# Order of the work in the first token group: rank sums ahead of the last adapter pieces, third x tile and table products earlier

## What is computed

```python
# layer 0: a channel mixing chosen per batch (64x64 weights applied to the token axis), then a dense layer
W = weights[condition]; h = einsum('bct,bcd->bdt', x, W)
base = einsum('bsd,od->bso', h, W_base) + b_base
decoded = (h @ enc0) @ (coefs0 * mask0) + (h @ enc1) @ (coefs1 * mask1)   # for each of 3 experts
transformed = real_fourier_orthogonal_multiply(decoded)                    # an inverse real Fourier transform
x = x + base + transformed.sum(axis=0) * 0.5
# layer 1: gated feed-forward, F = 2752, each product with a rank-16 adapter chosen per batch
act = silu(lora(x W_gate, A_gate, B_gate)) * lora(x W_up, A_up, B_up)
down = lora(act W_down, A_down, B_down)
x = x + down @ sign(weight).T + bias
```

## Time and profile before

| | us |
|---|---|
| median of 3 runs | 1940.22 (1938.87 to 1942.41) |
| the profiled execution's own time | 1939.48 |
| its span in the trace | 1937.8 |
| PE busy | 1912.8 (99%) |
| DVE busy | 1493.9 (77%) |
| ACT busy | 767.1 (40%) |
| POOL busy | 542.1 (28%) |

### The profile page before, as it was taken

How to read it: one execution, slowest core, us unless ns; L and a number is a source line. 1 busy time by engine, 2 the same in 40 slices (tenths; PEclk the granted TensorE clock), 3 DMA queues, 4 the chain that set the end, 5 groups by cost and what they waited for, 6 DMA issues and landing times.

```text
span 1937.8 us, 31530 instructions
## 1 busy us (share of the span) xinstructions
PE 1912.8 (99%) x9104; PEld 1608.2 (83%) x9104; DVE 1493.9 (77%) x2493; ACT 767.1 (40%) x1457; POOL 542.1 (28%) x935
## 2 busy tenths in 40 slices
PE   7899999999999999999999999999999999999998
PEld 6788888888988888888898888888889888888887
DVE  7877777778778777777777877777877787777786
ACT  4453333334344343333344434333335443334331
POOL 4542212213415212211523322212061322222100
PEclk9999999999999999999999999999999999999999
DMA  9755445543476554444447555554235655555411
GB/s 241 168 115 109 102 99 115 121 94 82 128 148 126 106 116 99 101 100 87 119 117 143 126 112 111 105 116 99 71 101 131 139 121 111 121 110 113 99 44 44
DMA packets 320629, 218.38 MB, mean 113 GB/s; under 512 B 177192, under 2 KB 311208, under 8 KB 320544
## 3 DMA queue, kind: packets, MB, share of 16 engines
q1 hardware_dynamic: 281952, 188.43, 43.2%
q0 software_dynamic: 36352, 24.19, 6.9%
q10 hardware_dynamic: 2240, 4.72, 0.7%
HBM read 204.35 MB, written 12.58 MB: 112 GB/s over the span
## 4 chain that ended last, share of the span: by engine, by line
PE 90%; DVE 4%; ACT 2%; issue 2%; SPq 1%; DMA 0%; DVEq 0%; ACTq 0%
PE ps L1517 26%; PE ps L1519 25%; PE ps L1518 25%; PE ps L1730 6%; PE ps L1657 2%; PE ps L1577 2%; PE ps L1578 2%; DVE ps L947 2%; PE ps L1543 1%; DVE split L933 1%; PE ps L1541 1%; PE ps L1596 1%; DMA base<-L_ffn_W_base 0%; ACT split L634 0%; ACT hidden L634 0%
## 5 line engine op out<-in xcount | busy, mean ns | idle before, releaser
L1517 PE MATMUL ps<-x,split 128*128 128x512 f32 x1376 | 538.8, 392 | 5.7 <-DVE act_f L1123 4.4
L1519 PE MATMUL ps<-x,split 128*128 128x512 f32 x1376 | 537.0, 390 | 0.0
L1518 PE MATMUL ps<-x,split 128*128 128x512 f32 x1376 | 536.2, 390 | 0.0
L634 ACT ACTIVATE split<-ps 128x512 fp32r<-128x512 f32 x344 | 203.1, 599 | 450.5 <-DVE ps L947 438.4
L526 POOL DMA_DIRECT2D nat_ad<-L_cond_A_down x224 | 136.9, 618 | 736.8 <-DVE ps L947 727.6
L1519 PEld LDWEIGHTS ps<-x,split 128*128 128x128 f32 x1376 | 258.8, 188 | 56.1
L1517 PEld LDWEIGHTS ps<-x,split 128*128 128x128 f32 x1376 | 259.5, 189 | 55.0 <-issue 4.8
L1518 PEld LDWEIGHTS ps<-x,split 128*128 128x128 f32 x1376 | 259.0, 188 | 54.9
L1517 PE MATMUL ps<-hidden 128*128 128x512 f32 x672 | 261.5, 389 | 0.0
L1518 PE MATMUL ps<-hidden 128*128 128x512 f32 x672 | 261.5, 389 | 0.0
L1519 PE MATMUL ps<-hidden 128*128 128x512 f32 x672 | 261.4, 389 | 0.0
(11 more groups left out here) (145 smaller groups left out, 2832.1 us busy)
## 6 DMA issues: line engine op xcount, KB each, us to landing
nat<-L_cond_W_gate SPq DMA_DIRECT2D x336, 128.0 KB
nat<-L_cond_W_up SPq DMA_DIRECT2D x336, 128.0 KB
nat_down<-L_cond_W_down SPq DMA_DIRECT2D x112, 384.0 KB, 6.4
nat_a<-L_ffn_weight SPq DMA_DIRECT2D x128, 128.0 KB, 2.8
nat<-effective_weight SPq DMA_DIRECT2D x24, 512.0 KB
nat<-x SPq DMA_DIRECT2D x16, 512.0 KB
nat_b<-L_cond_B_gate POOLq DMA_DIRECT2D x224, 24.0 KB, 2.2
nat_b<-L_cond_B_up POOLq DMA_DIRECT2D x224, 24.0 KB, 2.1
```

The costliest lines, as they stand in the source:

```text
L634: act.activation(dst, src, func).then_inc(piece_hi, 1)
L1517: pe.matmul(dst, a[0], b[0], start=first, stop=False)
L1518: pe.matmul(dst, a[0], b[1], start=False, stop=False)
L1519: return pe.matmul(dst, a[1], b[0], start=False, stop=last)
```

## The change

Four things are moved, all in the first group; no instruction is added or dropped.

1. SP issues the four loads of the Fourier table and the load of x tile 3 ahead of the six loads of the encoder.
2. ACT and DVE split x tile 2 ahead of the first mixing weights; the coefficient sums and their words come ahead of the first mixing unit's copies; the encoder's words come after x tile 3; `turn_base(1)` comes after the fourth pair of mixing weights, and mixing unit 2's copies after the low-rank words.
3. PE runs the table products ahead of mixing unit 2 instead of unit 3.
4. ACT and DVE do the rank sums after the pieces B 0 and B 1, ahead of B 2 and BREM.

```diff
@@ SP
             for i in range(2):
                 sp.dma_start(coef[i], ...)
                 sp.dma_start(coef_mask[i], ...)
-            for n in range(3):
-                sp.dma_start(enc[R0 * n:R0 * n + R0, :], enc0).then_inc(enc_in, 16)
-                sp.dma_start(enc[3 * R0 + R1 * n:3 * R0 + R1 * n + R1, :], enc1).then_inc(enc_in, 16)
             table_rows = fourier.rearrange("(p c) n -> p c n", c=KC)
             for i in range(4):
                 sp.dma_start(table[:, 2 * i:2 * i + 2], table_rows[:, 2 * i:2 * i + 2]).then_inc(table_in[i], 16)
             load_x(0, 3)
+            for n in range(3):
+                sp.dma_start(enc[R0 * n:R0 * n + R0, :], enc0).then_inc(enc_in, 16)
+                sp.dma_start(enc[3 * R0 + R1 * n:3 * R0 + R1 * n + R1, :], enc1).then_inc(enc_in, 16)
@@ ACT mixing_first
-                for p in range(2):
+                for p in range(3):
                     plain_unit(0, p, NAT_X + p, SPLIT_X + p)
                 for p in range(2):
                     cond(0, p)
-                plain_unit(0, 2, NAT_X + 2, SPLIT_X + 2)
+                low_rank_weights()
+                for e in range(2):
+                    mixing(0, e)
+                cond(0, 2)
+                plain_unit(0, 3, NAT_X + 3, SPLIT_X + 3)
                 act.wait_ge(enc_in, 96)
                 copy(enc_s.rearrange("r k (q d) -> r q k d", q=4),
                      enc.rearrange("r (q k d) -> r q k d", q=4, k=KC)).then_inc(enc_step, 1)
-                mixing(0, 0)
-                low_rank_weights()
-                mixing(0, 1)
-                cond(0, 2)
-                plain_unit(0, 3, NAT_X + 3, SPLIT_X + 3)
-                mixing(0, 2)
                 act.wait_ge(enc_step, 2)
                 act.wait_ge(g_psum, 1)
                 copy(enc[:, 0:512], ps[0:STACK, 6, :]).then_inc(g_moved, 1)
-                mixing(0, 3)
+                for e in range(2, 4):
+                    mixing(0, e)
                 cond(0, 3)
@@ ACT first_layer_all (making) and group
-                    lora_b_tiles(g, 0, "B", 0)
+                    lora_b_tiles(g, 0, "B", 0, range(2))
+                    ranks(g)
+                    lora_b_tiles(g, 0, "B", 0, range(2, PT))
...
-                ranks(g)
+                if g > 0:
+                    ranks(g)
@@ DVE mixing_first
-                for p in range(2):
+                for p in range(3):
                     plain_unit(0, p, NAT_X + p, SPLIT_X + p)
-                for p in range(2):
-                    cond(0, p)
-                plain_unit(0, 2, NAT_X + 2, SPLIT_X + 2)
+                cond(0, 0)
+                adapter_kept()
+                cond(0, 1)
                 adapter_sum()
-                mixing(0, 0)
-                enc_words()
-                mixing(0, 1)
+                for e in range(2):
+                    mixing(0, e)
                 cond(0, 2)
                 plain_unit(0, 3, NAT_X + 3, SPLIT_X + 3)
-                mixing(0, 2)
+                enc_words()
                 turn_base(0)
-                turn_base(1)
                 low_rank_out()
                 low_rank_words(0)
-                mixing(0, 3)
+                for e in range(2, 4):
+                    mixing(0, e)
                 cond(0, 3)
+                turn_base(1)
                 mixing(0, 4)
@@ DVE first_layer_first and group
-                lora_b_tiles(0, 0, "B", 0)
+                dve.wait_ge(nat_b_full, 256)
+                lora_b_turn(0, 0, "B", 0)
+                lora_b_turn(0, 0, "B", 1)
+                for j in range(2):
+                    lora_b_low(0, 0, "B", j)
+                ranks(0)
+                lora_b_turn(0, 0, "B", 2)
+                lora_b_low(0, 0, "B", 2)
                 lora_b_rest(0)
...
-                ranks(g)
+                if g > 0:
+                    ranks(g)
@@ PE mixing_all
-                    if e == 3 and making:
+                    if e == 2 and making:
                         low_rank_product()
```

More of the change, by code:

```diff
@@ L1308, in mixing_all, with adapter_kept @@
                         first_weight_unit(g, e // 2 - 1)
-            def adapter_sum():
+            def adapter_kept():
                 dve.wait_ge(coef_in, 64)
@@ L1314, in adapter_sum @@
                     dve.tensor_tensor(kept[i], coef[i], coef_mask[i], ALU.mult).then_inc(kept_step, 1)
+            def adapter_sum():
                 for i in range(2):
```

## The result

The changed kernel takes 1944.65 us (median of 11 runs, 1943.52 to 1945.69), the kernel before 1940.22 (11 runs): a ratio of 1.0022, 95% interval 1.0014 to 1.0030. It is slower by 4.4 us, outside my range. The profiled run took 1945.69 with a span of 1944.0, the longest of its 11; before's profiled run had a span of 1937.8.

A forecast was written before the change was run, and what follows sets the result against it. PE was taken to bound the kernel, with the DVE and ACT chain setting the head's end. Start -0.9, head +0.2, nothing after: -0.7 us, so a median of 1939.5 us, range 1936.8 to 1941.9.

The forecast's parts named there:

- the part on the start: Parts 1 to 3, up to the first weights: words and make_weights(0) 1.0 us sooner, moved loads hidden.
- I take it as hidden: Encoder load, some 5 us later behind table and tile 3: no cost, tile 3 on ACT covering the first microsecond otherwise.
- the sum of -0.9 at the start: Start, parts 1 to 3 together: 0.9 us gained, bounds -1.6 and +0.9.
- Rival C: Start: tile 2 late, first matmul up to 0.9 us later, or table loads delay first weights; 1941.3 us, chance 0.06.
- The head: Part 4, rank sums earlier: the DVE and ACT chain sets the end; +0.2 us, bounds -0.2 and +0.9.
- REM's stop: PE's wait ahead of REM's first product: shrinks from 4.41 to 0.6 us, with REM's products starting 3.8 us sooner.
- the new stop: PE's wait for BREM's lows ahead of the adapter products, 98.8 to 101.7: 2.9 us.
- ahead of U0: PE's further wait in the head after the adapter products and G0: about 1.4 us.
- ahead of the next G0: PE's stop at 136, ended by DVE: about 2 us where there were 0.31.
- chain: DVE and ACT handing pieces to each other through the head, up to G1's lows: 0.2 us later.
- Rival A: Head: PE's removed stop and slow products are worth their full 5.8 us; 1933.5 us, chance 0.08.
- Rival B: Head: clock falls at the new stops; a first fall is covered, a second costs 2.0 us; 1941.7 us, chance 0.11.

The follow-up runs named there:

- without part 1: The changed kernel with SP's loads in their old order, the encoder's ahead of the table's: 1939.70 us, ratio 1.0000.
- the pair out of the way: The changed kernel with ACT and DVE taking the third pair of mixing weights after x tile 3, the encoder's words and the base turn: 1938.71 us, ratio 0.9997.
- part 4 alone: The kernel before with only the rank sums moved ahead of B 2 and BREM: 1939.97 us, ratio 1.0001.
- the woven head: The changed kernel with loads in old order and B 2's and BREM's copies set between the steps of the rank sums: 1935.50 us, ratio 0.9981.
- half the table ahead: The changed kernel with two of the table's four loads ahead of the encoder's, the other two and x tile 3 behind: 1941.11 us, ratio 1.0008.
- one index read: The changed kernel with GpSimd reading all eight batch indices before the first weights' load, table loads still early: 1939.48 us, ratio 0.9999.
- GpSimd held: The changed kernel with loads in old order and two memsets on GpSimd ahead of the third pair's issue: 1946.02 us, ratio 1.0031.
- part 1 alone: The kernel before with only the table's four loads and x tile 3 moved ahead of the encoder's six: 1944.04 us, ratio 1.0020.
- U0 early: Woven-head kernel with x tile 2's split back behind two weight pairs, U0's turns around BREM's lows, its words before lora_t's: 1936.55 us, ratio 0.9985.

## Why the prediction was wrong

**The step that failed** is in the part on the start: "The table's loads and tile 3's come sooner, the encoder's later", which I put at nothing (of the encoder: "I take it as hidden"), and with it the sum of -0.9 at the start, where +5.57 was measured. I followed each moved load to the engine that uses its data. I did not ask what else goes through memory at that time. GpSimd's register reads are in no line of the diff, and I did not look at that engine's start, where its second issue has 5.42 us of idle time ahead of it. The price of this term is the 5.57 us at the mark. 2.99 of them are arrival: the pair's copy is 3.71 later, and `make_weights(0)` 2.99. The other 2.6 us are slow products behind the 3.84 us stop, in the profiled run; the profiled run is the longest of the 11, 1.0 us over their median. The mean clocks of the 11 lie between 0.996 and 0.998 and don't go with the times (the three at 0.998 took 1944.29, 1944.56 and 1945.24), so they don't tell whether every run lost these 2.6 us.

**Rival C** had the sign and half the words: "the table's loads hold up the first weights". The first weights were on time (the first matmul at 11.68 against 11.18, 0.5 us, inside my bound of 0.9). It was the third pair, and the price was not 0.9 but six times that, since a pair that PE does not need before 24.86 blocks what PE does need. I gave it 0.06 and stopped the range at 1941.9.

**What parts 2 and 3 are worth**: I had -0.9; without part 1 the mark moves by -0.51 (up to -0.9 against the other profiles with the old start). The read-out came at 23.72 and `make_weights(0)` at 26.68, where I had 23.4 and 26.3; the first matmul, which I had at no cost, is 0.34 later there. The mechanism was right and its size a little too good. With the pair out of the way the mark moves by -1.23, so the gain that I forecast was there, and was lost to the blocked queue.

**The head** came out by its steps. In the run of part 4 alone: REM's stop 0.64 us (forecast 0.6), the new stop 2.75 (2.9), 1.11 ahead of U0 (1.4), 1.38 ahead of the next G0 (2), chain +0.28 (+0.2). Rival A is refuted by the same run: a stop of 4.41 us was removed, and 1939.97 us stayed. The Trainium skill, Perfetto Trace Analysis, section Optimization Strategy, says to find the gaps on the engine in question and to make what ends them come sooner. Part 4 did that for the longest gap of the head and gained nothing; the woven head, which shortens the chain of DVE by 3.7 us against the change without part 1 and with it the stops that the chain ends ahead of the adapter products and of U0 (2.75 and 1.12 us become 0.26 in all), shows where a gain was to be had.

**Rival B**: the clock did fall once in the head, from 109 us in the changed kernel and from about 101 in the one with the pair behind. As reckoned there, a first fall is covered: with it the pair-behind kernel needs 1852.22 us from the mark to the end, and part 4 alone, at full clock, 1852.23. The changed kernel needs 0.4 more, and has no stop left ahead of the next G0. No second fall was seen: the granted clock is 1.00 in all stretches from 116 to 150.

## What to carry to other kernels

Before moving a load forward, list everything that goes to memory in those microseconds, register reads of indices on GpSimd above all, and what each engine has in line behind the data that they fetch. On engines that work in order, put a wait for data of uncertain arrival behind the work that does not need it, even if the data is usually there. And price a stop of the busiest engine by the chain that ends it: removing the stop is worth what the chain gets shorter, 0 us in one order of this head and 3 to 4 in another.

## What was not expected of the hardware

A register read of GpSimd from memory takes 0.92 us in the median of the changed kernel's nine pointer reads (0.99 before). The pointer and value reads that stand between the second and the third pair, begun at 5.8 to 6.2 us, took 3.3 to 4.7 us together in the eight kernels with the encoder's loads first, 5.81 with half the table ahead, and 6.69, 7.03, 7.08 and 7.20 with the whole table ahead. The DMA queues moved 2.95 MB between 5 and 15 us before, 3.56 MB after. The Trainium skill, DMA: Bandwidth & Descriptors, section Latency and other measured facts, gives a floor of about 600 ns for such a load; the quickest of the value's reads here took 527 ns, a little below it. Whether it is the amount in flight or the kind of load that counts was not separated.

The clock was less regular than I took it to be. After a stop of 2.75 us ahead of the adapter products, products ran at the full clock in the kernels of part 4 alone, of the change without part 1 and of one index read; after stops of 2.75 to 2.79 in the same place they ran slowly for a while in the change, with half the table, with GpSimd held and with the pair behind. A stop of 3.33 us ahead of the table products, in part 1 alone, left the clock at 1.00; one of 3.84 us ahead of `make_weights(0)` brought it down in the change, and one of 1.90 us ahead of the adapter products did with U0 early. What decides between them no run here shows.
